# Attention: the second projection of a step in one piece, and the product with v between the first two heads' transposes

## The reference, cut to what matters

```python
q = (Q @ Wq.T + bq).reshape(b, vc, h, hd)
k = (K @ Wk.T + bk).reshape(b, vc, h, hd)
v = (V @ Wv.T + bv).reshape(b, vc, h, hd)
atten = jnp.einsum('bqhd,bkhd->bhqk', q, k) / np.sqrt(hd)
atten = jax.nn.softmax(atten, axis=3)
out = jnp.einsum('bhqd,bdhv->bqhv', atten, v).reshape(b, vc, d_model)
return out @ Wo.T + bo
```

## Time and profile before

| | |
|---|---|
| time, median of 3 runs | 2803.12 us (2802.67 to 2806.06) |
| the profiled execution | 2806.08 us, its span from the first to the last instruction 2804.0 us |
| mean granted TensorE clock | 0.990 of full speed |
| busy over the span | TensorE matmuls 96%, weight loads 74%, VectorE 55%, ScalarE 37%, GpSimd 23% |
| DMA | 53 GB/s in the mean |
| attention stage | 1617 to 2297 us: TensorE busy 636.9 of 680 us, VectorE 501.1, ScalarE 368.3 |

### The profile page before, as it was taken

The page is one execution under the profiler, slowest core; times in us unless marked ns, Lnnn a source line. Parts: engine busy times, 40 slices in busy tenths (PEclk is TensorE's granted clock), DMA queues, the critical chain, the costliest instruction groups (busy, mean ns, idle before and its releaser), DMA issues.

```text
span 2804.0 us, 42177 instructions
## 1 busy us (share of the span) xinstructions
PE 2692.1 (96%) x15200; PEld 2082.5 (74%) x15200; DVE 1529.3 (55%) x2566; ACT 1029.9 (37%) x2385; POOL 638.3 (23%) x564
## 2 busy tenths in 40 slices
PE   6999999999999999999999989999999979999998
PEld 4777777777778888888888767777777756777775
DVE  6887887787785221233133477777777762111222
ACT  6244244344344222122212255555555543222221
POOL 0643543553451100010001011333222331000000
PEclk9999999999999999999999999999999989999999
DMA  3011011101113101110112120111011213211111
GB/s 134 16 46 45 8 37 45 36 9 45 45 46 137 61 0 60 60 60 14 46 60 94 37 100 9 53 60 60 22 45 60 79 46 125 86 45 45 45 45 45
DMA packets 85417, 147.81 MB, mean 53 GB/s; under 512 B 3968, under 2 KB 17920, under 8 KB 85344
## 3 DMA queue, kind: packets, MB, share of 16 engines
q1 hardware_dynamic: 85344, 146.84, 15.1%
HBM read 113.27 MB, written 33.55 MB: 52 GB/s over the span
## 4 chain that ended last, share of the span: by engine, by line
PE 84%; DVE 9%; issue 2%; ACT 2%; DMA 1%; POOL 1%; DVEq 0%; SPq 0%; POOLq 0%; ACTq 0%
PE ps L75 22%; PE ps L77 21%; PE ps L76 21%; PE ps L1640 4%; PE ps L1919 4%; PE ps L730 3%; PE ps L1652 2%; DVE mx_cv L537 2%; DVE at_pT L1504 1%; PE ps L1631 1%; DVE mx_m L545 1%; PE ps L706 1%; PE ps L718 1%; DVE at_r_hl L1511 1%; PE ps L1660 1%
## 5 line engine op out<-in xcount | busy, mean ns | idle before, releaser
L1354 ACT ACTIVATE at_pr<-ps,at_nm 128x256 f32<-128x256 f32 x512 | 236.4, 475 | 199.7 <-DVE at_nm L1498 199.7
L1056 DVE TENSOR_TENSOR gm_m_lo<-gm_m,gm_m_hi 128x512 fp32r<-128x512 f32 (+1 forms) x88 | 61.0, 693 | 416.9 <-ACT gm_m_hi L973 416.9
L75 PE MATMUL ps<-sh_u_hi,gm_gu_hi 128*128 128x512 f32 (+1 forms) x704 | 275.4, 391 | 1.6 <-DVE gm_gu_lo L213 1.6
L77 PE MATMUL ps<-sh_u_hi,gm_gu_lo 128*128 128x512 f32 (+1 forms) x704 | 275.3, 391 | 0.0
L76 PE MATMUL ps<-sh_u_lo,gm_gu_hi 128*128 128x512 f32 (+1 forms) x704 | 275.1, 391 | 0.0
L1504 DVE COPY at_pT<-ps 128x512 f32<-128x512 f32 x256 | 176.0, 687 | 129.3 <-PE ps L1640 125.0
L967 ACT ACTIVATE gm_sg<-ps 128x512 f32<-128x512 f32 (+1 forms) x88 | 52.6, 598 | 520.9 <-PE ps L77 520.9
L75 PE MATMUL ps<-sh_u_hi,qm_w_hi 128*128 128x512 f32 x512 | 201.4, 393 | 3.9 <-DVE qm_w_lo L211 3.9
L76 PE MATMUL ps<-sh_u_lo,qm_w_hi 128*128 128x512 f32 x512 | 199.9, 390 | 0.0
L77 PE MATMUL ps<-sh_u_hi,qm_w_lo 128*128 128x512 f32 x512 | 199.7, 390 | 0.0
L1640 PE MATMUL ps<-sh_ident,at_pr 128*128 128x128 f32 x1024 | 164.5, 284 | 35.0 <-DVE at_pT L1504 31.9
(11 more groups left out here) (237 smaller groups left out, 6322.9 us busy)
## 6 DMA issues: line engine op xcount, KB each, us to landing
sh_xf<-x_scratch SPq DMA_DIRECT2D x16, 1024.0 KB, 7.5
sh_xf<-in_x SPq DMA_DIRECT2D x8, 1024.0 KB, 7.3
mx_xr<-in_x SPq DMA_DIRECT2D x8, 1024.0 KB, 6.3
h_scratch<-mx_xr SPq DMA_DIRECT2D x8, 1024.0 KB, 5.2
sh_xf<-h_scratch SPq DMA_DIRECT2D x8, 1024.0 KB, 7.9
gm_xr<-in_x SPq DMA_DIRECT2D x8, 1024.0 KB, 7.3
gm_r<-h_scratch SPq DMA_DIRECT2D x8, 1024.0 KB, 5.9
x_scratch<-gm_r SPq DMA_DIRECT2D x8, 1024.0 KB, 5.1
```

Of the source, the lines that this page charges most:

```text
L75: nc.tensor.matmul(out, l_hi, r_hi, start=first, stop=False)
L77: return nc.tensor.matmul(out, l_lo, r_hi, start=False, stop=last)
L1354: A(pr[h][:, t, :], SC[h][:, SEQ * t:SEQ * t + SEQ], ACT.Exp, bias=nm[:, 4 * n + h, t:t + 1], accum_out=sums[:, 2 * b + t, 4 * g + h:4 * g ...
```

## The change

On TensorE, values of step n - 1 moves behind turn_p of head 0, and the first half of the second projection, with its waits, moves behind turn_p of head 1 and spread or turn, directly ahead of the second half. The order becomes: project slot 2n; turn_p head 0; values; turn_p head 1; spread or turn; project slot 2n + 1 in one piece; turn_p head 2; scores. On VectorE, take_pT of head 0 moves ahead of take of slot 2n. Nothing is added or removed.

```diff
--- before.py
+++ after.py
@@ -1530,9 +1530,9 @@
                 row_max(i, n, 3)
                 if n in TURN:
                     split_u(i + 1, TURN[n][0])
+                take_pT(i, n, 0)
                 if has(i, 2 * n, more):
                     take(i, 2 * n)
-                take_pT(i, n, 0)
                 take_pT(i, n, 1)
                 if n == 0 and not step_0(i):
                     normalise(i - 1, HG - 1)
@@ -1691,22 +1691,14 @@
                         pe.wait_ge(s["on"], HG * i + n // 2)
                     project(i, 2 * n, 0)
                     project(i, 2 * n, 1)
+                if step_0(i) and n == 0:
+
+                    pe.wait_ge(s["pout"], SL - AHEAD)
+                turn_p(i, n, 0)
                 if n > 0:
                     values(i, n - 1)
                 elif not step_0(i):
                     values(i - 1, QS - 1)
-                if step_0(i) and n == 0:
-
-                    pe.wait_ge(s["pout"], SL - AHEAD)
-                turn_p(i, n, 0)
-                if has(i, 2 * n + 1, more):
-                    if n == 0 and not step_0(i):
-                        pe.wait_ge(s["rte"], HG * i)
-                    elif n in TURN:
-                        pe.wait_ge(s["ulo"], KD * (i + 1 + B) + n)
-                    elif n in (2, 4, 6):
-                        pe.wait_ge(s["rte"], HG * i + n // 2)
-                    project(i, 2 * n + 1, 0)
                 turn_p(i, n, 1)
 
                 if n == 0 and not step_0(i):
@@ -1719,6 +1711,13 @@
                     pe.wait_ge(s["pout"], before(i, 2 * n + 1))
                     turn(i + 1, TURN[n][1])
                 if has(i, 2 * n + 1, more):
+                    if n == 0 and not step_0(i):
+                        pe.wait_ge(s["rte"], HG * i)
+                    elif n in TURN:
+                        pe.wait_ge(s["ulo"], KD * (i + 1 + B) + n)
+                    elif n in (2, 4, 6):
+                        pe.wait_ge(s["rte"], HG * i + n // 2)
+                    project(i, 2 * n + 1, 0)
                     project(i, 2 * n + 1, 1)
                 turn_p(i, n, 2)
                 pe.wait_ge(s["e"], 8 * QS * i + 8 * n + 8)
```

## The result

The changed kernel takes 2847.19 us (median of 4 runs, 2846.33 to 2851.01), the kernel before on the same chip 2804.57 (4 runs, 2802.67 to 2806.06): ratio 1.0155, 95% interval 1.0137 to 1.0173. It is 42.6 us slower; the forecast was 38 us slower (2841, range 2823 to 2863). The profiled execution after took 2846.84 us, its span 2844.8, at a mean granted clock of 0.991 (before 2806.08, 2804.0 and 0.990).

The account below looks back on a forecast made before the run. TensorE bounds the attention stage, busy 81.57 of 84.57 us per iteration. Added wait +8.5 less holes 3.1 gives +5.4, 32 over iterations 1 to 6, about +5.5 for 0 and 7: +38 on 2803.1, 2841 us, range 2823 to 2863.

Parts of the forecast that it names:

- Part 1, the holes that go: TensorE's idle time between the score matmuls and the fourth head's transposes, awaiting VectorE's copy, goes: -3.1 us per iteration.
- T0 to V: TensorE, from start of first head's transposes to start of the product with v: 0.43 us, between 0.35 and 0.53.
- V to C0: From start of the product with v to VectorE's copy of the first head's transposes, which awaits its end: 1.22 us.
- C0 to T1: From VectorE's copy of the first head's transposes to TensorE's transposes of the second head: 0.75 us.
- P to T0: TensorE, from start of the first projection (twelve matmuls) to the first head's transposes: 2.86 us.
- T1 to B or U: TensorE, from second head's transposes to the spread matmul or the transposes of x; inside 1.42 us from the first copy.
- Iterations 0 and 7: First and last attention iterations, where some steps lack a projection: together about +5.5 us, light steps gaining some 0.2 each.
- Holes that stay: Rival: idle time ahead of the fourth head's transposes remains, VectorE's third copy still being late: +62 us, 2865; chance 0.09.
- Cancelling: Rival: gain and loss cancel within 0.2%, by a cheaper switch to the product with v and shorter wait; chance 0.03.
- The clock falls: Rival: new holes in each step drop TensorE to half clock in a quarter of full steps: +77 on top, 2918; chance 0.06.
- Not slower: Rival: the first head's copy does not really wait for the product with v: -22 us over the stage, 2781; chance 0.10.
- the wait that is added: Product with v, VectorE's first copy and second head's transposes run in series, as the copy overwrites its input: +8.5 us per iteration.

Follow-up runs that it names:

- Experiment 7: Kernel before, with ScalarE's rounding of the last head group's output moved ahead of step 1's last exponentials, so GpSimd's subtraction comes earlier: 2798.52 us, ratio 0.998.
- Experiment 4: Changed kernel with VectorE's swap undone, the take of slot 2n again ahead of the copy of head 0's transposes: 2838.98 us, ratio 1.0122 to the kernel before.
- Experiment 3: Changed kernel, timing only: product with v reads head 1's probabilities for head 0's, so head 0's copy no longer waits for it: 2787.09 us, ratio 0.9934 to before.
- Experiments 1 and 2: Each one part of the change on the kernel before: first, only the half projection moved, 2842.79 us; second, only the product with v behind head 0's transposes, 2811.04 us.
- experiment 8: Kernel before with VectorE's small work, reciprocal transposes and ScalarE roundings moved, gathering and group 1's rounding put in step 6: 2777.22 us, ratio 0.9905.

## Why the prediction was right, point by point

The sign, the mechanism and the size held; the time is 6 us above the forecast of 2841 and inside the range; the profiled execution, forecast at 2844, took 2846.8.

- Part 1, the holes that go (-3.1 per iteration). Held: S to T3 is 0.91 or 0.92 in the steps of iteration 2 that had holes. The reason given for step 1 was incomplete: the 0.95 us there was put on the chain from U. Experiment 7 takes 0.81 of it away with U's chain as it was, by moving GpSimd's instruction off the cast. What the prediction called "the cast that varies" was most of the hole. The conclusion survived because the 1.39 us of cover is more than either cause.
- T0 to V, 0.43 between bounds 0.35 and 0.53. It is 0.53 in the full steps (0.52 in the one shown), the same as the switch to S. This term was mis-sized: I leaned to the row of a 128x512 matmul because V uses all 128 rows, but the switch to V's tile of 128x32 took what the switch to S's 32x128 takes. 0.10 in each of the 8 steps is 0.8 per iteration.
- V to C0, 1.22: 1.21. C0 to T1, 0.75: 0.75. P to T0, 2.86: 2.83 to 2.86. T1 to B or U, which the sum had at 0.67 (1.42 less 0.75): 0.60 to 0.66. T1 to P in steps 5 and 7, 0.41: 0.41. Twelve matmuls, 2.78: 2.75 to 2.77 behind B. Behind U they took 2.85 and U to P 0.42, where the sum had B's 2.78 and 0.32; it had left out the same in the time before, so this nearly cancels. From P to T2 the even steps grew by 1.15 to 1.20 (forecast 1.15), steps 1 and 3 by 1.13 and 1.11 (1.07), steps 5 and 7 by 0.91 and 0.96 (0.89), together 8.8 where the sum had 8.5; the holes gave back 3.1, as forecast, and T3 to U or R another 0.2 that nobody counted. So +5.4 per iteration was forecast and +5.50 measured: the 0.8 of T0 to V did not show in the total, since smaller errors lay against it, and that is luck.
- What lies behind the waiting C0 costs nothing, as said, but the take, which was in the sum. Experiment 4 gives it its own price, 8.2 us.
- Iterations 0 and 7: +5.5 forecast, about +8.3 measured (6.3 and 2). Step 0 of iteration 0 was forecast to gain 0.2 and took 16.17 us instead of 14.22, +1.95. It has no V, and I had not counted its new hole at T1 (0.87). The granted clock is 0.50 there from 1625 to 1631 us, the lower of its two levels, while before it was 0.50 from 1624.8 to 1628.2 and 1.00 from there to 1632, so more of the projection ran at the lower one. Step 4, where V itself runs at the lower clock (1.94 us instead of 1.07), grew by 0.92, no more than a full step. The light steps 2 and 3 gained nothing (-0.04 and +0.02) where -0.2 each was forecast.
- The total: +38 forecast against +40.8 in the two profiled spans, and iterations 0 and 7 hold nearly all of the difference (iterations 1 to 6: 32 against 32.2). The other 3 us of the 6 between 2841 and the median are no mechanism: the profiled execution of before lies 3.0 above the 2803.1 on which I forecast, that of after 0.35 below its median.
- The rivals. Holes that stay: out, S to T3 is 0.91. Cancelling: out. The clock falls: out in the full iterations, where it is 1.00 with 7.12 us idle in 90, and the mean is 0.991; what it did in iteration 0 is said above. The Trainium skill ("TensorE: Matmul & The Clock Gate", "HAM oscillation — how this bites in real kernels") tells of a kernel in which idle gaps between bursts of matmuls brought the clock down each time. Those gaps were longer than the holes here, and holes of 0.9 us in every step did not do so, so this case does not test it. Not slower: out, but for the reason given and no other. Experiment 3 realises it at 2787.1, against 2781 worked out; of the 6 us between, 0.8 per iteration is the step 5 hole that it left out.

What the prediction did not say is where the loss is decided. Its sum holds both causes, but its text speaks of the wait that is added. Experiments 1 and 2 part them: V's move with its added wait, the half projection in place, costs 6 us; the half taken away without the added wait costs 38. The wait decides only whether V can do the half's duty (experiment 3).

## What to carry to other kernels

Where one bank is filled and emptied in turn, the work between two fills is there to cover the copy (here 0.64 us until it starts and 0.75 until the bank is free): before moving it away, ask what stands in its place, and whether that work holds up the same copy through another buffer. The same wait cost at most 6 us with the half projection to cover it and 60 without (experiments 2 and 3), so price a move by the chain that is left and not by the wait that is new. When a short instruction lasts almost six times as long in one place as in another (0.98 and 0.17 us), look at the other engines in that window before looking for a cause in its inputs.

## What was not expected of the hardware

A VectorE cast of 128x16 from SBUF to SBUF takes 0.17 us. If it starts while GpSimd runs a 128x512 subtraction, it ends about 0.03 us after GpSimd's instruction does: 0.98 at the end of step 1 of the kernel before, 1.13 in step 5 of experiment 3. The subtraction with two SBUF inputs of the same 16 columns does so as well (0.17 to 1.21). The reciprocal at 1805.04, which started 0.04 us behind GpSimd's instruction, took its usual 0.24. In step 3 of iteration 2 of the kernel before the cast takes 0.40, to 1828.06, with GpSimd's end at 1828.03. VectorE at the end of that iteration, and GpSimd:

```profile
1867.49 0.69 DVE L1504 COPY at_pT<-ps 128x512 f32<-128x512 f32 x1 [1.13 <-PE ps L1640]
...
1868.38 0.17 DVE L1511 CAST at_r_hl<-at_rinv 128x16 fp32r<-128x16 f32 x1
```
```profile
1867.20 1.28 POOL L1434 TENSOR_TENSOR at_o_lo<-at_o,at_o_hi 128x512 fp32r<-128x512 f32 x1 [8.23 <-ACT at_o_hi L1371]
```

A copy out of PSUM, wholly under GpSimd's instruction, keeps its 0.69. The cast that starts 0.1 us before GpSimd's end (1868.48) keeps its 0.17; by the rule above it could not end before 1868.51, and by its own time it ends at 1868.55, so the two agree. Nor does every GpSimd instruction do this: in experiment 8 the cast at 1773.82 and the subtraction at 1774.03 ran wholly under one that multiplies and subtracts by scalars (TENSOR_SCALAR, 128x512, 1772.62 to 1774.70) and took 0.17 each. Experiment 7 shows the cause by moving GpSimd's instruction, and the ScalarE rounding ahead of it, off the cast. The Trainium skill, "GPSIMD Engine Reference", "8. Key points", names contention between the two engines at their shared SBUF interfaces for VectorE instructions in a 2-port perf mode or with two SBUF inputs. The rows agree for the subtraction, which has two SBUF inputs. The cast has one, and no run here shows whether it runs in such a mode. In these rows the short instruction waits for the end of the long one.
